# Scores turned as two rounded parts and spread in one pass, in the second edge stage of a two-layer graph network

## The reference

```python
key_e = k_rel[edge_type, edge_src]
val_e = v_rel[edge_type, edge_src]
att = (q[edge_dst] * key_e).sum(-1) * rel_pri[edge_type] / jnp.sqrt(jnp.float32(dk))
seg = edge_dst * r + edge_type
amax = jax.ops.segment_max(att, seg, num_segments=S)
ex = jnp.exp(att - amax[seg])
denom = jax.ops.segment_sum(ex, seg, num_segments=S)
w = ex / denom[seg]
hsum = jax.ops.segment_sum(w[:, :, None] * val_e, seg, num_segments=S)
```

## Time and profile before

| what | value |
|---|---|
| median of 3 runs | 3666.56 us (3665.77 to 3671.32) |
| the profiled execution | 3659.42 us |
| its span, first to last instruction | 3657.6 us |
| PE busy in the span | 3381.2 us, 92% |
| DVE busy | 3185.6 us, 87% |
| ACT busy | 2594.7 us, 71% |
| POOL busy | 2390.0 us, 65% |
| mean granted TensorE clock | 0.974 |

### The profile page before, as it was taken

How to read it: one execution, slowest core, us unless ns; L and a number is a source line. 1 busy time by engine, 2 the same in 40 slices (tenths; PEclk the granted TensorE clock), 3 DMA queues, 4 the chain that set the end, 5 groups by cost and what they waited for, 6 DMA issues and landing times. The chain is left out here.

```text
span 3657.6 us, 111781 instructions
## 1 busy us (share of the span) xinstructions
PE 3381.2 (92%) x25829; PEld 2771.8 (76%) x25830; DVE 3185.6 (87%) x9898; ACT 2594.7 (71%) x7607; POOL 2390.0 (65%) x2549
## 2 busy tenths in 40 slices
PE   3979999999999997996999999999999999997997
PEld 2547777777777775775888888888888888886996
DVE  6768999999999995664999999999999999996775
ACT  1856777777777774543878888888888888884553
POOL 3756777777777763554666666666666666663775
PEclk8989999999999997998999999999999999998998
DMA  3979999999999984776888888888888888884663
GB/s 102 263 230 309 301 296 301 298 298 298 299 298 300 300 253 165 276 258 224 254 235 239 240 236 239 237 239 237 238 238 239 238 237 239 236 237 150 213 208 126
DMA packets 604966, 898.40 MB, mean 246 GB/s; under 512 B 208971, under 2 KB 418646, under 8 KB 604371
## 3 DMA queue, kind: packets, MB, share of 16 engines
q0 software_dynamic: 164240, 566.71, 50.5%
q1 hardware_dynamic: 440643, 330.78, 30.2%
HBM read 724.25 MB, written 175.28 MB: 246 GB/s over the span
## 5 line engine op out<-in xcount | busy, mean ns | idle before, releaser
L1595 POOL DMA_INDIRECT kv1c<-kv_table,rec x900 | 865.9, 962 | 299.0 <-issue 284.6
L916 POOL DMA_INDIRECT kv<-kv_table,rec x832 | 848.3, 1020 | 282.3 <-issue 258.2
L1700 DVE CUSTOM_DVE_ANT_0 masked_scores<-score_p,far 126x384 f32<-126x384 f32 x1200 | 595.6, 551 | 30.2 <-issue 14.1
L1640 ACT ACTIVATE wv<-kv1c,wv 128x64 f32<-128x64 f32 x2400 | 605.9, 335 | 17.7
L954 ACT ACTIVATE gates<-gates_p 128x512 f32<-128x512 f32 x832 | 448.3, 591 | 77.5 <-PE gates_p L1087 77.5
L1803 PE MATMUL sum_p<-wv,hot 128*126 128x260 f32 x1800 | 477.7, 402 | 1.4 <-ACT wv L1640 1.4
L1759 PE MATMUL qe_p<-qrel,hotT 126*128 126x256 f32 x1800 | 443.0, 382 | 22.7 <-ACT hotT L1625 18.1
L1107 PE MATMUL sum_p<-msg,hot_weighted 128*124 128x256 f32 x1664 | 416.2, 393 | 5.3 <-ACT hot_weighted L962 5.3
L1759 PEld LDWEIGHTS qe_p<-qrel,hotT 126*128 126x128 f32 x1800 | 343.7, 191 | 74.9 <-ACT hotT L1625 18.7
L1107 PEld LDWEIGHTS sum_p<-msg,hot_weighted 128*124 128x124 f32 x1664 | 295.2, 187 | 116.2 <-issue 73.9
L1803 PEld LDWEIGHTS sum_p<-wv,hot 128*126 128x126 f32 x1800 | 316.1, 189 | 76.1 <-ACT wv L1640 1.8
(11 more groups left out here) (285 smaller groups left out, 7392.0 us busy)
## 6 DMA issues: line engine op xcount, KB each, us to landing
key<-segment_keys SPq DMA_DIRECT2D x300, 192.0 KB
q_blk<-q_table SPq DMA_DIRECT2D x208, 256.5 KB
acc_table<-acc SPq DMA_DIRECT2D x300, 130.0 KB
qrel<-q_by_relation SPq DMA_DIRECT2D x300, 128.0 KB
feat<-in_edge_feat_t SPq DMA_DIRECT2D x208, 128.0 KB
agg_and_x_plus_h<-total SPq DMA_DIRECT2D x208, 128.0 KB
kv1c<-kv_table,rec POOLq DMA_INDIRECT x900
kv<-kv_table,rec POOLq DMA_INDIRECT x832
```

Source lines behind the costliest of these rows:

```text
L916: pool.indirect_dma_start(kv[it.slot(AHEAD)][:, t, :], None, c["kv0_d"], bass.IndirectOffsetOnAxis(ap=rec[k][:, t, 0:1].bitcast(I32), axis ...
L1595: pool.indirect_dma_start(kv[k][:, t, :], None, c["kv1_d"], bass.IndirectOffsetOnAxis(ap=rec[k][:, t, 0:1].bitcast(I32), axis=0)).then_inc ...
L1640: ins = act.activation(wv[k][:, t, h, 0:DK], kv[s][:, t, D + h * DK:D + (h + 1) * DK], ACT.Copy, scale=wv[k][:, t, h, DK:DK + 1])
L1700: dve.tensor_tensor_reduce(junk[k][:, h], score_p[:, :, h, :], far[it.slot(U1)][:], 1.0, FLOOR, ALU.subtract, ALU.max, top[s][:, h:h + 1]) ...
```

## The change

The score's tile is one of its own now. ACT rounds it into lanes 0 to 3 (`score_lead`, first in ACT's list), DVE writes the difference, rounded too, into lanes 4 to 7 (`score_rest`, behind `maxima`), and PE's transpose waits for the second of them. `spread_head` has a second row of ones for each head, so that the matmul adds the two parts again, and both its operands are F32R, which runs as one pass. The sum old peak + par is computed once (`old_peak`) into a tile `old`; `new_peak` and `peak_drop` read that tile, and the loads of chunk + 6 wait for it instead of for `drop`. The core of the diff:

```diff
-        spread_head = sb("spread_head", [T1 * LANE, HEADS, SEG])
+        spread_raw = sb("spread_head_raw", [T1 * LANE, HEADS, SEG])
+        spread_head = sb("spread_head", [T1 * LANE, HEADS, SEG], F32R)
-        score = [t[:, :, 0:HEADS] for t in lanes]
-        scoreT = [sb(f"scoreT{k}", [T1 * LANE, P]) for k in range(2)]
+        score = [sb(f"score{k}", [P, T1, HEADS]) for k in range(U1)]
+        scoreT = [sb(f"scoreT{k}", [T1 * LANE, P], F32R) for k in range(2)]
+        old = [sb(f"old{k}", [SEG, HEADS]) for k in range(U1)]
...
-                    wait(sp, drop_ready, it, U1)
+                    wait(sp, old_ready, it, U1)
...
+                def score_lead(it):
+                    k = it.slot(U1)
+                    wait(act, score_ready, it)
+                    wait(act, score_turned, it, U1)
+                    act.copy(lanes[k][:, :, 0:HEADS].bitcast(F32R), score[k][:]).then_inc(lead_ready, 1)
...
-                run_chunks(act, steps, ((4, weights), (4, weigh), (2, scoreT_out), (0, distances), (0, transposed_hot),
+                run_chunks(act, steps, ((2, score_lead), (4, weights), (4, weigh), (2, scoreT_out), (0, distances), (0, transposed_hot),
...
+                dve.wait_ge(const_loaded, 16 * T1)
+                dve.tensor_copy(spread_head[:], spread_raw[:]).then_inc(filled, 1)
...
+                def score_rest(it):
+                    k = it.slot(U1)
+                    wait(dve, lead_ready, it)
+                    dve.tensor_tensor(lanes[k][:, :, HEADS:2 * HEADS].bitcast(F32R), score[k][:], lanes[k][:, :, 0:HEADS],
+                                      ALU.subtract).then_inc(rest_ready, 1)
...
+                def old_peak(it):
+                    s = it.slot(U1)
+                    wait(dve, drop_ready, it, U1)
+                    wait(dve, peak_ready, it, 1)
+                    dve.tensor_tensor(old[s][:], peak[it.prev().slot(U1)][:],
+                                      par[s][0:SEG, 2:3].to_broadcast([SEG, HEADS]), ALU.add).then_inc(old_ready, 1)
...
-                    dve.scalar_tensor_tensor(peak[s][:], peak[it.prev().slot(U1)][:], par[s][0:SEG, 2:3], top[s][:],
-                                             ALU.add, ALU.max).then_inc(peak_ready, 1)
+                    dve.scalar_tensor_tensor(peak[s][:], top[s][:], FLOOR, old[s][:], ALU.max,
+                                             ALU.max).then_inc(peak_ready, 1)
...
-                    dve.scalar_tensor_tensor(drop[s][:], peak[it.prev().slot(U1)][:], par[s][0:SEG, 2:3], peak[s][:],
-                                             ALU.add, ALU.subtract).then_inc(drop_ready, 1)
+                    dve.tensor_tensor(drop[s][:], old[s][:], peak[s][:], ALU.subtract).then_inc(drop_ready, 1)
...
-                run_chunks(dve, steps, ((2, q_times_k), (4, below_peak), (2, scores), (4, cap), (3, maxima),
-                                        (4, weigh_last), (3, new_peak), (5, add_acc), (3, peak_drop)), U1)
+                run_chunks(dve, steps, ((2, q_times_k), (3, old_peak), (4, below_peak), (2, scores), (4, cap), (3, maxima),
+                                        (2, score_rest), (4, weigh_last), (3, new_peak), (5, add_acc), (3, peak_drop)), U1)
...
-                pe.wait_ge(const_loaded, 16 * T1)
                 pe.wait_ge(filled, FILLS)
...
-                    wait(pe, score_ready, it)
+                    wait(pe, rest_ready, it)
                     wait(pe, scoreT_ready, it, 1)
...
-        spread_head[h, h, :] = 1.0
+        spread_head[[h, HEADS + h], h, :] = 1.0
```

More of the change, by code:

```diff
@@ L1500, in edges_1 @@
         qe_ready, qk_ready, score_ready = sem("qe1"), sem("qk1"), sem("score1")
+        lead_ready, rest_ready = sem("score_lead"), sem("score_rest")
         score_turned, scoreT_ready, spread_ready = sem("score_turned"), sem("scoreT_ready"), sem("score_spread")
-        top_ready, peak_ready, drop_ready = sem("top_ready"), sem("peak_ready"), sem("drop_ready")
+        top_ready, old_ready, peak_ready, drop_ready = sem("top_ready"), sem("old_ready"), sem("peak_ready"), sem("drop_ready")
         of_edge_ready, diff_ready, capped_ready = sem("peak_of_edge"), sem("diff_ready"), sem("capped_ready")
@@ L1507, in edges_1 @@
         stored, held = sem("acc_stored"), sem("edge1_held")
-        LOADS, FILLS = 4, 2 * U1 + 1
+        LOADS, FILLS = 4, 2 * U1 + 2
         with nc.Block() as block:
@@ L1513, in _ @@
                 for t in range(T1):
-                    sp.dma_start(spread_head[t * LANE:(t + 1) * LANE, :, :], w0["spread_head"]).then_inc(const_loaded, 16)
+                    sp.dma_start(spread_raw[t * LANE:(t + 1) * LANE, :, :], w0["spread_head"]).then_inc(const_loaded, 16)
                 steps = chunk_steps(sp, c["steps1"])
@@ L1685, in scores @@
                     wait(dve, diff_ready, it, U1)
-                    dve.tensor_reduce(score[it.slot(U1)], qk[it.slot(2)][:], AX, ALU.add).then_inc(score_ready, 1)
+                    dve.tensor_reduce(score[it.slot(U1)][:], qk[it.slot(2)][:], AX, ALU.add).then_inc(score_ready, 1)
+                def score_rest(it):
[3 more added lines that the diff above has]
+                                      ALU.subtract).then_inc(rest_ready, 1)
                 def maxima(it):
@@ L1699, in maxima @@
                     for h in range(HEADS):
-                        dve.tensor_tensor_reduce(junk[k][:, h], score_p[:, :, h, :], far[it.slot(U1)][:], 1.0, FLOOR,
+                        dve.tensor_tensor_reduce(junk[k][:, h], score_p[:, :, h, :], far[it.slot(U1)][:], 1.0, -BIG,
                                                  ALU.subtract, ALU.max, top[s][:, h:h + 1]).then_inc(top_ready, 1)
+                def old_peak(it):
[4 more added lines that the diff above has]
+                                      par[s][0:SEG, 2:3].to_broadcast([SEG, HEADS]), ALU.add).then_inc(old_ready, 1)
                 def new_peak(it):
                     s = it.slot(U1)
+                    wait(dve, old_ready, it)
                     wait(dve, top_ready, it, per=HEADS)
-                    wait(dve, peak_ready, it, 1)
                     wait(dve, of_edge_ready, it, U1)
-                    dve.scalar_tensor_tensor(peak[s][:], peak[it.prev().slot(U1)][:], par[s][0:SEG, 2:3], top[s][:],
-                                             ALU.add, ALU.max).then_inc(peak_ready, 1)
+                    dve.scalar_tensor_tensor(peak[s][:], top[s][:], FLOOR, old[s][:], ALU.max,
+                                             ALU.max).then_inc(peak_ready, 1)
                 def peak_drop(it):
@@ L1720, in below_peak @@
                     wait(dve, capped_ready, it, 2)
-                    dve.tensor_tensor(diff[it.slot(2)][:], score[it.slot(U1)], peak_p[:],
+                    dve.tensor_tensor(diff[it.slot(2)][:], score[it.slot(U1)][:], peak_p[:],
                                       ALU.subtract).then_inc(diff_ready, 1)
```

## The result

The changed kernel is slower: 3705.1 us median of 5 runs (3697.1 to 3731.0), against 3666.56 us (3665.77 to 3671.32); the ratio is 1.0111, with a 95% interval of 1.0082 to 1.0139. The forecast was 3635 with a range up to 3696, so it lies outside, on the side of the rivals. Of these the least likely one came true, the clock.

What follows compares the result with a forecast made beforehand. PE, DVE, their loop and the gather loop stood close together; afterwards the gather was to bound: (11.82 + 3.50) / 3 = 5.11, plus 0.05 noise, 5.16 against 5.27: -33 us, +2 at the start, so 3635 us, range 3592 to 3696.

Steps and rivals of the forecast that it cites:

- the clock: Rival: PE idles some 0.6 us a chunk, a tenth of the stage runs at 1.2 GHz; near 3750 us; 3%.
- The period: Time per chunk in the second edge stage: 5.16 us against 5.27 before, over 300 chunks.
- the gather loop: Three periods from q_times_k through fade and POOL's gather issue to the landing: 11.82 + 3.50, or 5.11 us a period.
- the noise: Period above the limiting loop from varying landings: 0.25 us a chunk before, 0.05 taken after.
- The longer chain: PE's transpose waits for score_rest behind the maxima, so fade ends 7.13 us after q_times_k instead of 6.48, 0.65 later.
- The spread: On PE, 12 of 24 passes go; 12 x 0.038 = 0.46 us, saving 0.45 and lowering PE's floor to 4.55.
- The rival that one pass is no cheaper: On PE, an F32R pass costs as much as two; maxima loop 5.27, with noise 5.35; 3693 us; 8%.
- DVE: Four new or changed small instructions at 0.08 us each, 0.32 against 0.28; DVE's floor from 4.79 to 4.83.
- SP's loads: Issued 3.8 us sooner, they meet the gather's transfer less; landing 3.50 us after the third issue instead of 3.90.
- The start: At the stage's start POOL and PE wait for DVE's copy of the constants; 2 us taken, between nothing and 3.9.
- The slower rival by the wait: Transpose behind the maxima lengthens the gather loop; landing 4.12, period 5.36 us, 3696 us in all; 13%.
- The rival of more: Gather landing 3.1 us and no noise: period 4.97, at most -90 + 2, near 3590 us; 11%.

Runs made afterwards that it cites:

- `score_rest` moved: The changed kernel with score_rest between the second and third of the four maxima instead of behind the fourth: 3643.6 us, 0.9957 of the kernel before.
- the two changed kernels nearly without falls: The changed kernel with six useless transposes a chunk on PE, 3633.5 us (0.9932), and the changed kernel with the spread in two fp32 passes, 3635.0 us (0.9935).
- the one pass alone: The kernel before with scoreT and spread_head in F32R, score not split, no score_rest or old_peak: 3667.1 us, ratio 1.0015.

## Why the prediction was wrong, step by step

**The step that failed is the clock.** The sum has no term for it: it takes the full clock for the whole steady part, and the rival that says otherwise got 3%. What set that chance is the sentence "in the steady part the clock was 1.00". That row is of a PE that was busy 97% of the time, and says nothing of one with 10% idle. The only fall weighed was one behind 18 us of idleness. The runs showed 14.5% of the steady part at 1.2 GHz with 0.51 us of idle time a chunk. With the pause filled, by useless transposes or by the second pass, the falls all but go and the ratio drops from 1.0111 to 0.9932 and 0.9935, which is 64 to 66 us. The forecast's own ratio was 0.9914, so without the falls the rest of the sum would have come within some 0.2%, in part by luck, as said below.

The mechanism was seen in advance, and the idle time of 0.6 was near. Its price of 117 us for a tenth of the stage is only roughly borne out. Filling the pause gave back 64 to 66 us, which is a lower bound, since the filling costs something too. The profile allows 0.14 to 0.42 us a chunk (5.49 against 5.35 or 5.07), or 42 to 126 us, for 14.5%.

The prediction took from the Trainium skill, TensorE: Matmul & The Clock Gate, section HAM oscillation, that pauses between bursts of matmuls can bring the clock down, and the traces agree. From 2000 to 3200 us the longest pause of PE before was 0.76 us, and the clock never fell; the changed kernel has 49 pauses of over 1 us and 33 falls. The waits in the page's own example are longer than any pause here, the longest of which is 2.09 us, and one long pause isn't needed either: with `score_rest` moved there are 23 falls and no pause over 0.88 us.

**The period** was forecast as 5.16. Off the low clock it is 5.07 to 5.35 by the cut, so that number is neither borne out nor refuted; the two changed kernels nearly without falls have 5.18 and 5.20. The terms of the gather loop are nearer than they deserve. The median end of `fade` is 7.03, forecast 7.13, and (7.03 + 0.27 + 4.42 + 3.42) / 3 = 5.05, forecast 5.11. In the two kernels nearly without falls the period lies 0.11 and 0.13 above the same loop (their medians are 7.21 and 7.17, their landings 3.28 and 3.22), so the noise was more than the 0.05 that was taken.

**The longer chain was mis-sized, because one step was read as typical.** The prediction has `fade` at 6.48 before and 0.65 later after. The median before was 6.95 and after 7.03, 0.08 later. The parts show why: the one pass alone brings it from 6.95 to 6.57, and the place of `score_rest` takes 0.46 of that back, since with `score_rest` moved it is 6.57 again. By this reading a full PE held up the transpose before, and now the wait does. With 6.95 the gather loop before is 5.18, and the noise on it was 0.09, not 0.25. In the steps shown, the transpose's load to ACT's copy took 0.72 us, not 0.92. Behind the 0.92 were 0.21 between load and matmul in the step of the earlier trace rows, where PE was still busy with the queries; in the step shown above both start together.

**The spread**: 0.66 us for 12 passes, 0.27 of it the last, so 0.035 a pass; taken 0.038. The rival that one pass is no cheaper is out.

**DVE**: the new and changed small instructions stand 0.07 to 0.08 apart, as taken from `cap`; a step without waits is 4.77, forecast 4.83.

**SP's loads**: `rec` is issued 1.28 after `q_times_k` (3183.87), forecast 1.3. The landing is 3.34 on average and with DVE's 0.08 that is 3.42, forecast 3.50. The correlation was a cause: with the loads back behind `drop` it is 3.76, with the old peak alone on the kernel before 3.25. So moving the loads was worth 0.42 to 0.57 us of landing. The rule of turns between queues that the prediction took from the Trainium skill, DMA: Bandwidth & Descriptors, section Queues, rings and completion order, names no size, and no run here shows whether the turns are what did it.

**The start**: +2 was taken for the copy of the constants. Of the eight kernels that copy the constants, six start their first `q_times_k` between 1720 and 1726 us, the changed one at 1733.8 and the one with two passes at 1746.4; the kernel before starts it at 1724.6. The six show no cost of the copy; what held up the other two was not looked into. In the changed kernel's profiled execution it is 9 us.

**The slower rival by the wait** had the right sign by the wrong route: it needed landings of 3.84 and more, and they were 3.34. **The rival of more** has a slip: 3659.4 - 90 + 2 + 7.1 is 3579, not 3590.

So the account of the change, in steps that were each run. The old peak's own tile wins 42 us, as the part alone shows (1.15%), or 0.11 us a chunk in the profile. How much of it is the sooner landing and how much the cheaper instructions on DVE was not separated. The split of the scores with its wait, still spread in two passes, gives 18 of them back (0.9885 to 0.9935). The one pass on top of it lets the clock fall and costs 64 (0.9935 to 1.0111). That adds up to some 40 us of loss, as measured. By the intervals each part is good to some 10 us.

## What to carry to other kernels

In this kernel, work taken off TensorE was no gain, because the pauses that it left lowered the clock. When a nearly full TensorE is relieved in a stage that another chain holds at the same period, ask first what fills the pause, and read the granted clock of a busy stage as holding for that busyness alone. A cheap test is to put useless work into the pause: if the kernel gets faster and the granted clock rises with it, the clock was the cause.

Read a chain's length as a median over many chunks. One step from the timeline was 0.47 us quicker than the typical one here, and so a chain that grew by 0.08 us was forecast to grow by 0.65.

When several limits stand together, look at what one edit brings along: here the part worth having was the old peak's own tile, with its early release of a load's buffer and its cheaper instructions, and not the one in the title.

## What the hardware showed that was not expected

The granted clock fell to 1.2 GHz with TensorE busy 91% of the time in all and no pause over 2.09 us; with `score_rest` moved, 23 times with no pause over 0.88. Over the ten kernels the share of low clock rose nearly in step with PE's idle time, from 0 to 3% in those with 0.08 to 0.19 us a chunk to 10 to 15% in those with 0.45 to 0.52. In one stretch the falls came every 24 us. That a fall makes chunks late and so feeds the next one is a reading of this pattern, which no run tested.

The time at which another queue's loads are issued moved the landing of a gather by 0.4 to 0.6 us, at much the same load of the DMA engines, 80 to 85%.
